# Attention in a macaron block: the probability-value product issued as two halves of 256 query columns

## The chip, the cores and the metric

The kernel runs on one core of one Trainium2 chip. The metric is the device time of the whole program in microseconds (us), the median of several runs. Engines are written as the profile writes them: PE is TensorE's matmul side and PEld its weight load, DVE is VectorE, ACT is ScalarE, POOL is GpSimd and SP is SyncE, which here only issues DMAs.

## The reference

The program is six stages over 16 sequences of 512 tokens, each token a row of 256 floats: feed-forward, gated linear attention, feed-forward, mixture of experts, **softmax attention with 16 heads**, mixture of experts. Only the fifth stage is touched:

```python
q = q.reshape(B, S, 16, 16).transpose(0, 2, 1, 3)      # k, v alike
scores = jnp.einsum('bhsd,bhtd->bhst', q, k) / math.sqrt(16)
scores = scores + _band_mask(S, scores.dtype)          # 0.1 where |s - t| <= 2
attn = jax.nn.softmax(scores, axis=-1)
out = jnp.einsum('bhst,bhtd->bhsd', attn, v)
```

followed by the output projection and the residual sum.

## The kernel before

The attention stage is `att_stage` (line 962). Every engine has its own instruction stream, written out by hand, and semaphores tie the streams together. All streams loop over the 16 sequences with `over_sequences`: the first and the last sequence are written out, the 14 between them are a loop. One sequence is 16 **steps** (`st`), four heads by one tile of 128 keys; four steps make a **group** of four heads (`GROUPS`, `GH`, `TILES` are all 4). A step is four **pairs** (`i` = 0 to 3, one for each head). A pair on PE is

- `s2_unit` (matmul on line 1229): the transposed scores, 128 keys by 512 queries, of this step, into one of two PSUM buffers `s2_`. It waits until ACT has read the buffer of the head two before;
- `s1_unit` (line 1217): scores of the step seven ahead (`AHEAD`), wanted only for their row maximum, into one of two buffers `s1_`. It waits until DVE has read the buffer two before.

ACT takes the exponential of every `s2_` buffer into `prob` (`exp_unit`, line 1382), DVE the maximum of every `s1_` buffer (`max_unit`, line 1476). When the four exponentials of a step are there, POOL multiplies the band's factor into them (`band_factor`, line 1134). The **product** `pv` (matmul on line 1250) then multiplies the four heads' probabilities (128 keys by 512 queries each, float32) by their values and a column of ones, 32 columns of weights for each head, each head in its own quarter of the PE's columns, so that the four run beside each other. It accumulates over the four steps of a group in the bank `pv`. The product of step `st - 1` stands behind pair 3 of step `st`:

```python
if i == 3 and st:
    pv(b, st - 1)
```

`prob` has two buffers; `exp_unit` of pair 0 waits for the product of two steps before. After a group ACT copies `pv` out (`ot_copy`, line 1362, at pair 0 of steps 1, 5, 9, 13), PE transposes it (`out_t`, line 1263) and DVE normalises it.

Between the pairs PE also does the projections of the next sequence and of the last one, at places given by tables of (step, pair): `XT_AT` transposes, `QK_AT` the projections of queries and keys (line 1189, three matmuls at each place: one in step 3, three in 4, three in 8, one in 9), `OT_AT` and `Y_AT` the output projection (steps 6, 10, 11), `V_AT` the values (line 1198, six matmuls at each place: steps 13, 14, and two in 15). In a pair these come behind the product. The projected queries and keys go through ACT (`k_full`, `high_part`), POOL (`low_part`, line 1143) and SP (`write`, line 1064) to DRAM, and from there back into stacks (`load`, line 1075). The row maxima of a group are transposed (`max_t`, line 1239, at pair 1 of steps 1, 5, 9, 13), copied by ACT and put into the query stack by a DMA (`max_row`, line 1080); pair 0 of steps 0, 4, 8 and 12 waits for it. On SP's queue the `max_row` for step 8 stands behind the `write` of the next sequence's first half, and the one for step 12 behind the `write` of its second half.

Of the kernel before, what the change touches and what calls it, by code (L numbers as in the profile page):

```python
# [17 lines left out]
TILES = TOKENS // P  # L18
DM = 256
# [927 lines left out]
HD = DM // HEADS  # L947
GROUPS, GH = 4, 4
STEPS = GROUPS * TILES
# [12 lines left out]
def att_stage(core, a, name):  # L962
# [6 lines left out]
    nc, s = core.nc, core.sem  # L969
    SCALE = HD ** -0.5  # L970
    WIDE = P + 2 * BAND
    with ExitStack() as ctx:
# [22 lines left out]
        vaug = core.sbuf("v_ones", [P, TILES, HEADS, 2 * HD], F32, ctx)  # L995
        prob = core.sbuf("prob", [P, 2, GH, TOKENS], F32, ctx)
# [9 lines left out]
        pvp = core.psum("pv", [P, TOKENS], ctx)  # L1006
# [12 lines left out]
        band_done = s(name + "_band_done")  # L1019
        pv_done = s(name + "_pv_done")  # L1020
# [5 lines left out]
        ot_ready = s(name + "_ot_ready")  # L1026
# [8 lines left out]
        v_ready = s(name + "_v_ready")  # L1035
# [6 lines left out]
        first = lambda b: isinstance(b, int) and b == 0  # L1042

        with nc.Block() as block:
# [121 lines left out]
            def _(pe):  # L1166
                pe.wait_ge(spread_done, 2)
                n = 0
                for x, w in ((bvs, "h"), (bvs, "l"), (bvl, "h")):
                    for k in range(KT):  # L1170
                        op = nc.tensor.matmul(tpy[:, 0, :], x[:, k, :], (wh if w == "h" else wl)["o"][:, k, :],
                                              start=(n == 0), stop=(n == 5))
# [4 lines left out]
                def qk_proj(b, m, parts=range(4), after_o=False):  # L1177

                    if parts[0] == 0 and m == 0:
                        pe.wait_ge(norm.xl_ready, b + 1)  # L1180
                    elif parts[0] == 0:
                        pe.wait_ge(full_ready, 2 * (KT * b + m))
                        if after_o:
                            pe.wait_ge(ol_ready, b - 1)
                    for part in parts:
                        x, k = part // 2, part % 2
                        n = "qk"[x]
                        for i, (w, act) in enumerate([(wh, core.xh), (wl, core.xh), (wh, core.xl)]):
                            op = nc.tensor.matmul(tp[:, x, :], w[n][:, k, m * P:(m + 1) * P], act[:, k, :],
                                                  start=(k == 0 and i == 0), stop=(k == KT - 1 and i == 2))  # L1190
                    if parts[-1] == 3:
                        op.then_inc(qk_ps, 1)
# [17 lines left out]
                def s1_unit(b, st, i):  # L1210

                    g, qt = st // TILES, st % TILES
                    if qt == 0 and i == 0:
                        pe.wait_ge(loaded[g], PER_LOAD * b + PER_LOAD)
                    pe.wait_ge(max_done, (b * STEPS + st) * GH + i + 1)
                    r = slice(0, MAX_ROW)
                    nc.tensor.matmul(s1p[i % 2][:, :], qs[r, g, i, qt * P:(qt + 1) * P], ks[r, g, i, :],  # L1217
                                     start=True, stop=True).then_inc(s1_ready, 1)

                def s2_unit(b, st, i):  # L1220

                    g, kt = st // TILES, st % TILES
                    if kt == 0 and i == 0:
                        pe.wait_ge(rowed[g], 16 * b + 16)
                    pe.wait_ge(exp_done, (b * STEPS + st) * GH + i + 1)
                    r = slice(0, MAX_ROW + 1)
                    nc.tensor.matmul(s2p[i % 2][:, :], ks[r, g, i, kt * P:(kt + 1) * P], qs[r, g, i, :],  # L1229
                                     start=True, stop=True).then_inc(s2_ready, 1)  # L1230

                def max_t(b, g):
                    pe.wait_ge(max_done, (b * GROUPS + g) * TILES * GH + TILES * GH + 2)

                    if first(b) and g in (1, 2):
                        pe.wait_ge(nmt_ready, g)
                    elif not (first(b) and g == 0):
                        pe.wait_ge(on_ready, b * GROUPS + g - 2)
                    nc.tensor.transpose(mp[0:TILES * GH, 0:P], nm[:, g % 2, :, :].rearrange("p h t -> p (h t)"),
                                        core.ident[:, :]).then_inc(nm_ready, 1)  # L1240

                def pv(b, st):
                    g, kt = st // TILES, st % TILES
                    pe.wait_ge(band_done, b * STEPS + st + 1)
                    if st == 0:
                        pe.wait_ge(v_ready, b + 1)
                    if kt == 0 and not (first(b) and g == 0):
                        pe.wait_ge(ot_ready, b * GROUPS + g)
                    for i in range(GH):
                        op = nc.tensor.matmul(pvp[2 * HD * i:2 * HD * (i + 1), :], vaug[:, kt, GH * g + i, :], prob[:, kt % 2, i, :],  # L1250
                                              start=(kt == 0), stop=(kt == TILES - 1))
                    op.then_inc(pv_done, 1)

                def out_t(b, g):

                    pe.wait_ge(ot_ready, b * GROUPS + g + 1)

                    if isinstance(b, int) and b == core.batches - 1 and g >= 2:
                        pe.wait_ge(on_ready, b * GROUPS + g)
                    else:  # L1260
                        pe.wait_ge(nmt_ready, b * GROUPS + g + 3)
                    for qt in range(TILES):
                        op = nc.tensor.transpose(mp[:, qt * P:(qt + 1) * P], ot[:, qt * P:(qt + 1) * P], core.ident[:, :])
                    op.then_inc(tr_ready, 1)
# [11 lines left out]
                def o_project(b, t):  # L1276
                    if t == 0:
                        pe.wait_ge(ol_ready, b + 1)
                    tokens(t, oh, ol, "o", y_ps)
# [12 lines left out]
                def body(b, before, more):  # L1292
                    for st in range(STEPS):
                        ahead = st + AHEAD
                        for i in range(GH):
                            s2_unit(b, st, i)
                            if ahead < STEPS:
                                s1_unit(b, ahead, i)
                            elif more:
                                s1_unit(b + 1, ahead - STEPS, i)  # L1300

                            at = (st, i)
                            if i == 3 and st:
                                pv(b, st - 1)
                            elif i == 3 and before:
                                pv(b - 1, STEPS - 1)
                            if st % TILES == 1 and i == 1:
                                if st + TILES < STEPS:
                                    max_t(b, st // TILES + 1)
                                elif more:  # L1310
                                    max_t(b + 1, 0)
                            if st % TILES == 2 and i == 0:
                                if st > 2:
                                    out_t(b, st // TILES - 1)
                                elif before:
                                    out_t(b - 1, GROUPS - 1)
                            if more and at in XT_AT:
                                n = XT_AT.index(at)
                                norm.transpose(pe, b + 1, lambda: pe.wait_ge(v_ready, b + 1), range(n, n + 1))
                            if more and at in QK_AT[0]:  # L1320
                                n = QK_AT[0].index(at)
                                qk_proj(b + 1, 0, range(n, n + 1))
                            if more and at in QK_AT[1]:
                                n = QK_AT[1].index(at)
                                qk_proj(b + 1, 1, range(n, n + 1), before)
                            if before and at in OT_AT:
                                if more:
                                    o_transpose(b - 1, OT_AT.index(at), full_ready, 2 * (KT * b + KT + 1))
                                else:
                                    o_transpose(b - 1, OT_AT.index(at), v_ready, b + 1)  # L1330
                            if before and at in Y_AT:
                                o_project(b - 1, Y_AT.index(at))
                            if more and at in V_AT:
                                v_proj(b + 1, V_AT.index(at), before)

                over_sequences(pe, core.batches, body)
                last = core.batches - 1
                pv(last, STEPS - 1)
                out_t(last, GROUPS - 1)
                for k in range(KT):  # L1340
                    o_transpose(last, k, *((y_ready, last + 1) if last else (v_ready, 1)))
# [880 lines left out]
```

## Time and profile before

| | us |
|---|---|
| median of 3 runs (4211.86 to 4222.06) | 4212.57 |
| the profiled execution's own time | 4213.35 |
| its span, first to last instruction | 4211.6 |
| attention: from the first s2 matmul (2177.6) to the last (3439.5) | 1262 |
| one sequence in the middle of it, by its 16 steps | 79.2 |
| PE busy over the whole span | 3768.9 (89%) |

A row of the timeline has the start in us, the duration in us, engine, line, operation, tiles and shapes, and, where the engine had been idle, how long and what ended it. A matmul's duration overlaps the next one's, so the distance from start to start tells what a matmul costs. A float32 matmul of the product appears as two records. The granted TensorE clock (PEclk) is either 1.00 (2.4 GHz) or 0.50 (1.2 GHz); a mean between them is a stretch with both.

### The profile page before, as it was taken

How to read it: one execution, taken by the hardware profiler on the slowest of the kernel's cores; microseconds unless marked ns; L12 is line 12 of the kernel's file. 1: busy time of each engine (PE TensorE's matmuls, PEld its weight loads, DVE VectorE, ACT ScalarE, POOL GpSimd, SP SyncE). 2: the span in 40 equal slices, each digit the busy share in tenths (PEclk: the TensorE clock that was granted, in tenths of full speed). 3: DMA queues.
4: the chain of work that ended last, by engine and by line, in shares of the span. 5: the costliest groups of instructions: out<-in, count | busy, mean ns of one | idle time of the engine just before them, and what ended most of it. 6: DMA issues, size and time to landing. Idle time of an engine off the chain costs nothing. (4 is left out here: it accounts for less than half of the span.)

```text
span 4211.6 us, 79961 instructions
## 1 busy us (share of the span) xinstructions
PE 3768.9 (89%) x27516; PEld 2923.9 (69%) x27516; DVE 2720.6 (65%) x5626; ACT 1790.0 (43%) x3205; POOL 1364.4 (32%) x1045
## 2 busy tenths in 40 slices
PE   6997888887997999999968899998999979999999
PEld 4886677776886888888734455554555538888888
DVE  5665677775676566666655666666676655666665
ACT  3444344443554333333325555555555553333333
POOL 2555222222665222222222323323323322222222
PEclk9998999998998999999969999999999989999999
DMA  3000000000001000000034334333333410000000
GB/s 101 0 0 14 2 0 0 0 0 1 0 0 38 1 0 0 0 0 0 10 69 90 76 67 90 83 68 86 86 68 83 90 46 6 15 10 10 15 10 16
DMA packets 72273, 131.72 MB, mean 31 GB/s; under 512 B 7776, under 2 KB 40944, under 8 KB 66048
## 3 DMA queue, kind: packets, MB, share of 16 engines
q1 hardware_dynamic: 72192, 130.65, 13.2%
q8 instruction: 49, 0.80, 0.1%
q14 instruction: 32, 0.26, 0.0%
HBM read 71.38 MB, written 58.72 MB: 31 GB/s over the span
## 5 line engine op out<-in xcount | busy, mean ns | idle before, releaser
L1476 DVE TENSOR_REDUCE neg_max_sb<-s_ps 128x1 f32<-128x512 f32 x1024 | 689.5, 687 | 436.0 <-PE s_ps L1217 433.1
L1382 ACT ACTIVATE prob_sb<-s_ps 128x512 f32<-128x512 f32 x1024 | 599.8, 599 | 543.4 <-PE s_ps L1229 532.7
L850 POOL TENSOR_TENSOR m_act_lo_sb<-m_act_sb,m_act_hi_sb 128x512 fp32r<-128x512 f32 x320 | 414.1, 1294 | 1042.1 <-ACT m_act_hi_sb L816 1042.1
L806 ACT ACTIVATE m_silu_sb<-moe_h_ps 128x512 f32<-128x512 f32 x320 | 191.4, 598 | 966.7 <-PE moe_h_ps L761 966.7
L1229 PE MATMUL s_ps<-q_stack_sb,k_stack_sb 97*128 97x512 f32 x1024 | 483.3, 473 | 101.5 <-DMA q_stack_sb<-neg_max_t_sb 87.2
L1134 POOL TENSOR_TENSOR prob_sb<-prob_sb,band_sb 128x520 f32<-128x520 f32 (+1 forms) x256 | 285.2, 1114 | 853.0 <-ACT prob_sb L1382 852.9
L904 DVE TENSOR_TENSOR m_act_sb<-moe_h_ps,m_silu_sb 128x512 f32<-128x512 f32 x320 | 220.6, 689 | 502.1 <-ACT m_silu_sb L806 472.4
L1229 PEld LDWEIGHTS s_ps<-q_stack_sb,k_stack_sb 97*128 97x128 f32 x1024 | 203.0, 199 | 409.4 <-ACT prob_sb L1382 239.1
L1217 PE MATMUL s_ps<-k_stack_sb,q_stack_sb 96*128 96x512 f32 x1024 | 451.8, 444 | 28.7 <-DMA k_stack_sb<-qk_scratch 16.3
L529 POOL TENSOR_TENSOR f_sq_lo_sb<-f_sq_sb,f_sq_hi_sb 128x512 fp32r<-128x512 f32 x256 | 329.6, 1296 | 349.8 <-ACT f_sq_hi_sb L504 349.7
L916 DVE SCALAR_TENSOR_TENSOR x_resident_sb<-moe_y_ps,gates_sb,x_resident_sb 128x256 f32 (+1 forms) x1024 | 422.5, 474 | 0.5
L779 PE MATMUL moe_y_ps<-w2h_sb,m_act_hi_sb 128*128 128x256 f32 x1280 | 367.2, 287 | 12.3 <-DVE x_resident_sb L916 10.0
L779 PE MATMUL moe_y_ps<-w2h_sb,m_act_lo_sb 128*128 128x256 f32 x1280 | 358.4, 280 | 0.0
L779 PE MATMUL moe_y_ps<-w2l_sb,m_act_hi_sb 128*128 128x256 f32 x1280 | 358.4, 280 | 0.0
L499 ACT ACTIVATE f_relu_sb<-ffn_hp_ps 128x512 f32<-128x512 f32 x256 | 153.4, 599 | 314.1 <-PE ffn_hp_ps L452 313.6
L1250 PE MATMUL pv_ps<-prob_sb,v_ones_sb 128*32 128x512 f32 x2048 | 282.1, 624 | 3.5 <-POOL prob_sb L1134 1.5
L1217 PEld LDWEIGHTS s_ps<-k_stack_sb,q_stack_sb 96*128 96x128 f32 x1024 | 208.1, 203 | 100.5 <-DVE neg_max_sb L1476 50.6
L779 PEld LDWEIGHTS moe_y_ps<-w2h_sb,m_act_hi_sb 128*128 128x128 f32 x1280 | 240.6, 188 | 37.1 <-DVE x_resident_sb L916 21.0
L761 PE MATMUL moe_h_ps<-xnT_hi_sb,w1h_sb 128*128 128x512 f32 x640 | 259.9, 406 | 4.7 <-DVE xnT_lo_sb L158 4.7
L566 DVE TENSOR_TENSOR f_sq_sb<-ffn_hp_ps,f_relu_sb 128x512 f32<-128x512 f32 x256 | 174.8, 687 | 134.3 <-ACT f_relu_sb L499 99.2
L761 PE MATMUL moe_h_ps<-xnT_hi_sb,w1l_sb 128*128 128x512 f32 x640 | 259.4, 405 | 0.0
L761 PE MATMUL moe_h_ps<-xnT_lo_sb,w1h_sb 128*128 128x512 f32 x640 | 257.9, 403 | 0.0
(282 smaller groups left out, 8904.4 us busy)
## 6 DMA issues: line engine op xcount, KB each, us to landing
qk_scratch<-qk_hi_sb SPq DMA_DIRECT2D x128, 256.0 KB
q_stack_sb<-qk_scratch SPq DMA_DIRECT2D x64, 384.0 KB, 5.2
k_stack_sb<-qk_scratch SPq DMA_DIRECT2D x64, 384.0 KB, 7.0
qk_scratch<-qk_lo_sb SPq DMA_DIRECT2D x64, 256.0 KB
x_resident_sb<-x SPq DMA_DIRECT2D x4, 2048.0 KB, 17.8
out<-x_resident_sb SPq DMA_DIRECT2D x16, 512.0 KB, 2.9
moe_w_values_sb<-routed_w SPq DMA_DIRECT2D x12, 512.0 KB, 6.5
moe_w_values_sb<-shared_w SPq DMA_DIRECT2D x6, 256.0 KB, 5.4
```

Of the source, the lines that this page charges most:

```text
L529: nc.gpsimd.tensor_tensor(sql[:, j, :], sq[:, j % 2, :], as_f32(sqh[:, j, :]), ALU.subtract).then_inc(low_ready, 1)
L761: op = nc.tensor.matmul(out[e % 2][:, :], w[:, e, k, :], x[:, k, :], start=(k == 0 and i == 0), stop=(k == KT - 1 and i == 2))
L779: op = nc.tensor.matmul(y[:, t, :], x[:, slot(e), t * P:(t + 1) * P], w[:, e, :], start=(e <= EXPERTS and t % 2 == 0 and i == 0), stop=(i ...
L850: nc.gpsimd.tensor_tensor(al[:, slot(e), :], act_f[:, e % 2, :], as_f32(ah[:, slot(e), :]), ALU.subtract).then_inc(low_ready, 1)
L904: nc.vector.tensor_tensor(act_f[:, e % 2, :], h3[e % 2][:, :], silu[:, e % 2, :], ALU.mult).then_inc(act_ready, 1)
L916: op = nc.vector.scalar_tensor_tensor(xt, y[:, t, :], gain, xt, ALU.mult, ALU.add)
L1134: nc.gpsimd.tensor_tensor(pr, pr, bcast(band[:, off:off + hi - lo].unsqueeze(1), [P, GH, hi - lo]), ALU.mult).then_inc(band_done, 1)
L1217: nc.tensor.matmul(s1p[i % 2][:, :], qs[r, g, i, qt * P:(qt + 1) * P], ks[r, g, i, :], start=True, stop=True).then_inc(s1_ready, 1)
L1229: nc.tensor.matmul(s2p[i % 2][:, :], ks[r, g, i, kt * P:(kt + 1) * P], qs[r, g, i, :], start=True, stop=True).then_inc(s2_ready, 1)
L1250: op = nc.tensor.matmul(pvp[2 * HD * i:2 * HD * (i + 1), :], vaug[:, kt, GH * g + i, :], prob[:, kt % 2, i, :], start=(kt == 0), stop=(kt ...
L1382: nc.scalar.activation(prob[:, kt % 2, i, :], s2p[i % 2][:, :], ACT.Exp).then_inc(exp_done, 1)
L1476: nc.vector.tensor_reduce(nm[:, g % 2, i, qt:qt + 1], s1p[i % 2][:, :], AXIS_X, ALU.max, negate=True).then_inc(max_done, 1)
```

## The change

The product is issued in two calls. The first, `half` 0, takes query columns 0 to 255 and stands behind pair 2; the second, columns 256 to 511, stands behind pair 3. The waits are on the first call, the semaphore increment on the second. Each call has four matmuls of 256 columns where there were four of 512. The accumulation's start flag is set by the first half of a group's first step only.

```diff
-                def pv(b, st):
+                def pv(b, st, half):
                     g, kt = st // TILES, st % TILES
-                    pe.wait_ge(band_done, b * STEPS + st + 1)
-                    if st == 0:
-                        pe.wait_ge(v_ready, b + 1)
-                    if kt == 0 and not (first(b) and g == 0):
-                        pe.wait_ge(ot_ready, b * GROUPS + g)
+                    c = slice(half * DM, half * DM + DM)
+                    if half == 0:
+                        pe.wait_ge(band_done, b * STEPS + st + 1)
+                        if st == 0:
+                            pe.wait_ge(v_ready, b + 1)
+                        if kt == 0 and not (first(b) and g == 0):
+                            pe.wait_ge(ot_ready, b * GROUPS + g)
                     for i in range(GH):
-                        op = nc.tensor.matmul(pvp[2 * HD * i:2 * HD * (i + 1), :], vaug[:, kt, GH * g + i, :], prob[:, kt % 2, i, :],
-                                              start=(kt == 0), stop=(kt == TILES - 1))
-                    op.then_inc(pv_done, 1)
+                        op = nc.tensor.matmul(pvp[2 * HD * i:2 * HD * (i + 1), c], vaug[:, kt, GH * g + i, :],
+                                              prob[:, kt % 2, i, c], start=(kt == 0 and half == 0),
+                                              stop=(kt == TILES - 1), skip_group_check=True)
+                    if half:
+                        op.then_inc(pv_done, 1)
...
-                            if i == 3 and st:
-                                pv(b, st - 1)
-                            elif i == 3 and before:
-                                pv(b - 1, STEPS - 1)
+                            if i >= 2 and st:
+                                pv(b, st - 1, i - 2)
+                            elif i >= 2 and before:
+                                pv(b - 1, STEPS - 1, i - 2)
```

On PE, in step 4 of a middle sequence, from pair 2 to the first score matmul of step 5, the program before has (s_0 and s_1 are the two buffers of either kind of scores, tp is the projection's bank):

```order
L1229 MATMUL s_0_ps<-q_stack_sb,k_stack_sb 128x512
L1215 REGISTER_ALU
L1217 MATMUL s_0_ps<-k_stack_sb,q_stack_sb 128x512
L1189 MATMUL tp_ps<-xnT_hi_sb,Wk_hi_sb 128x512
L1189 MATMUL tp_ps<-xnT_hi_sb,Wk_lo_sb 128x512
L1189 MATMUL tp_ps<-xnT_lo_sb,Wk_hi_sb 128x512
L1227 REGISTER_ALU
L1229 MATMUL s_1_ps<-q_stack_sb,k_stack_sb 128x512
L1215 REGISTER_ALU
L1217 MATMUL s_1_ps<-k_stack_sb,q_stack_sb 128x512
L1250 MATMUL pv_ps<-prob_sb,v_ones_sb 32x512 x4
```

At the same place on PE the changed program has (line 1252 is the product's matmul there):

```order
L1229 MATMUL s_0_ps<-q_stack_sb,k_stack_sb 128x512
L1215 REGISTER_ALU
L1217 MATMUL s_0_ps<-k_stack_sb,q_stack_sb 128x512
L1252 MATMUL pv_ps<-prob_sb,v_ones_sb 32x256 x4
L1189 MATMUL tp_ps<-xnT_hi_sb,Wk_hi_sb 128x512
L1189 MATMUL tp_ps<-xnT_hi_sb,Wk_lo_sb 128x512
L1189 MATMUL tp_ps<-xnT_lo_sb,Wk_hi_sb 128x512
L1227 REGISTER_ALU
L1229 MATMUL s_1_ps<-q_stack_sb,k_stack_sb 128x512
L1215 REGISTER_ALU
L1217 MATMUL s_1_ps<-k_stack_sb,q_stack_sb 128x512
L1252 MATMUL pv_ps<-prob_sb,v_ones_sb 32x256 x4
```

The first half has moved ahead of the third place's projection and of pair 3; the second half stands where the whole product stood. No other engine's stream is changed.

## Rows read from the trace of the kernel before

**Rows 1.** The page: PE's busy time, and the product's group of instructions.

```profile
PE 3768.9 (89%) x27516; PEld 2923.9 (69%) x27516; DVE 2720.6 (65%) x5626; ACT 1790.0 (43%) x3205; POOL 1364.4 (32%) x1045
...
L1250 PE MATMUL pv_ps<-prob_sb,v_ones_sb 128*32 128x512 f32 x2048 | 282.1, 624 | 3.5 <-POOL prob_sb L1134 1.5
```

**Rows 2.** Timeline of PE alone, end of step 14 and start of step 15.

```profile
2815.16 0.40 PE L1229 MATMUL s_ps<-q_stack_sb,k_stack_sb 97*128 97x512 f32 x1
2815.40 0.39 PE L1217 MATMUL s_ps<-k_stack_sb,q_stack_sb 96*128 96x512 f32 x1
2815.72 1.06 PE L1250 MATMUL pv_ps<-prob_sb,v_ones_sb 128*32 128x512 f32 x8
2816.72 0.50 PE L1229 MATMUL s_ps<-q_stack_sb,k_stack_sb 97*128 97x512 f32 x1
2817.06 0.39 PE L1217 MATMUL s_ps<-k_stack_sb,q_stack_sb 96*128 96x512 f32 x1
```

**Rows 3.** Timeline of a step with nothing but pairs and product (last sequence).

```profile
3395.79 0.61 PE L1250 MATMUL pv_ps<-prob_sb,v_ones_sb 128*32 128x512 f32 x4
...
3396.33 0.50 PE L1229 MATMUL s_ps<-q_stack_sb,k_stack_sb 97*128 97x512 f32 x1
...
3396.87 2.34 ACT L1382 ACTIVATE prob_sb<-s_ps 128x512 f32<-128x512 f32 x4 [1.18 <-PE s_ps L1229]
...
3397.10 2.57 DVE L1476 TENSOR_REDUCE neg_max_sb<-s_ps 128x1 f32<-128x512 f32 x4 [0.97 <-PE s_ps L1217]
...
3397.52 0.50 PE L1229 MATMUL s_ps<-q_stack_sb,k_stack_sb 97*128 97x512 f32 x1
...
3397.86 0.49 PE L1217 MATMUL s_ps<-k_stack_sb,q_stack_sb 96*128 96x512 f32 x1
...
3398.18 0.39 PE L1229 MATMUL s_ps<-q_stack_sb,k_stack_sb 97*128 97x512 f32 x1
...
3398.45 0.49 PE L1217 MATMUL s_ps<-k_stack_sb,q_stack_sb 96*128 96x512 f32 x1
...
3398.87 1.06 PE L1250 MATMUL pv_ps<-prob_sb,v_ones_sb 128*32 128x512 f32 x8
...
3399.87 0.50 PE L1229 MATMUL s_ps<-q_stack_sb,k_stack_sb 97*128 97x512 f32 x1
```

**Rows 4.** Busy time by step: steps 0, 1, 3, 4, 12, 14, and all 16 summed.

```profile
2742.07:2745.93 3.86, 3.61 (x20) 1.58 (x16) 3.08 (x6) 2.18 (x4) 1.53 (x2) 1.00 0.96 170
2745.93:2750.51 4.58, 4.20 (x25) 2.02 (x22) 3.88 (x7) 3.83 (x10) 0.67 (x2) 1.00 0.09 14
...
2754.45:2759.20 4.75, 4.54 (x24) 2.07 (x20) 4.20 (x8) 2.52 (x5) 1.57 (x2) 1.00 0.00 0
2759.20:2764.38 5.18, 5.18 (x29) 3.29 (x25) 2.96 (x5) 2.92 (x5) 1.10 (x2) 1.00 0.00 0
...
2803.79:2808.37 4.58, 4.58 (x16) 2.15 (x16) 2.77 (x4) 2.39 (x4) 0.99 (x1) 0.63 0.85 152
...
2812.50:2816.72 4.22, 4.22 (x31) 2.70 (x27) 3.30 (x7) 2.28 (x4) 1.10 (x2) 1.00 0.00 0
...
sum 79.16, PE 72.02 PEld 40.45 DVE 53.15 ACT 44.83 POOL 24.92; mean PE 4.50 PEld 2.53 DVE 3.32 ACT 2.80 POOL 1.56
```

**Rows 5.** Timeline of PE: first matmuls of steps 8 and 12, and a wait in step 9.

```profile
2779.97 0.50 PE L1229 MATMUL s_ps<-q_stack_sb,k_stack_sb 97*128 97x512 f32 x1 [2.66 <-DMA q_stack_sb<-neg_max_t_sb]
...
2787.47 0.50 PE L1217 MATMUL s_ps<-k_stack_sb,q_stack_sb 96*128 96x512 f32 x1 [0.29 <-DMA k_stack_sb<-qk_scratch]
...
2803.79 0.50 PE L1229 MATMUL s_ps<-q_stack_sb,k_stack_sb 97*128 97x512 f32 x1 [2.60 <-DMA q_stack_sb<-neg_max_t_sb]
```

**Rows 6.** Timeline of SP's DMA issues in steps 6 and 7.

```profile
2771.89 3.13 SPq L1064 DMA_DIRECT2D qk_scratch<-qk_lo_sb  x2
2775.15 0.96 SPq L1080 DMA_DIRECT2D q_stack_sb<-neg_max_t_sb  x1
```

**Rows 7.** Timeline of POOL: the band factor of step 5, in step 6.

```profile
2770.65 1.13 POOL L1134 TENSOR_TENSOR prob_sb<-prob_sb,band_sb 128x528 f32<-128x528 f32 x1
```

In rows 4 the columns are the stretch in us, its length, the busy us of PE, PEld, DVE, ACT and POOL with the number of instructions of each, the granted clock, the share of the DMA engines and GB/s.

More of the change, by code:

```diff
@@ L1337, in _ @@
                 last = core.batches - 1
-                pv(last, STEPS - 1)
+                pv(last, STEPS - 1, 0)
+                pv(last, STEPS - 1, 1)
                 out_t(last, GROUPS - 1)
```

## The prediction

> **What bounds the kernel now.** The page first: PE is busy 89% of the span, and the product has 282.1 us of it in 2048 records [rows 1]. That says where the change sits, not what it is worth, so next the attention stage step by step. The busy times by step [rows 4] show PE at 72.02 us of a sequence's 79.16, and two kinds of step: in steps 4 and 14 PE is busy from end to end, in steps 0 and 1 it isn't, and DVE and ACT have extra work. Then the timeline at the steps' ends. The reader should see two things there. First, around each product PE takes longer than its columns need [rows 2]. Second, steps 8 and 12 begin with a wait of 2.66 and 2.60 us for the DMA that brings the row maxima [rows 5], and this DMA stands on SP's queue behind the write of the next sequence's projections [rows 6]. What PE does in the steps just before such a wait is hidden by it; what it does elsewhere sets the time.
>
> **What a product costs PE, whole and halved.** Start to start, an ordinary score matmul takes 0.24 us (2815.16 to 2815.40). Around the product: 0.32 from the last s1 matmul to the product, 1.00 from there to the next s2 matmul, and 0.34 from that to its s1 matmul, whose weight load isn't hidden as usual [rows 2]. Together 1.66, less the 0.48 of two ordinary distances: a whole product costs 1.18 us. Its second record begins 0.54 before the next s2 matmul (3395.79 to 3396.33) [rows 3], so the first pass over 512 columns takes 1.00 - 0.54 = 0.46. The second pass streams as many columns, of which half are to go as well; it is drawn at 0.43 here, a little under the first (its start isn't delayed by a weight load). A half product then streams about 0.43 us less than a whole one: 1.00 - 0.43 = **0.57 from its start to the next s2 matmul**. Everything else around it comes once for each call: 0.32 + 0.57 + 0.34 - 0.48 = 0.75. Two halves cost 1.50 where the whole cost 1.18: **+0.32 us a step where PE sets the pace**. No trace of before shows 256 columns. The bound below is that all of the 1.00 halves (0.50, and 2 x 0.68 = 1.36: +0.18). The bound above is that nothing but the first pass's 0.46 and half as much of the second go (0.65: +0.4 or more); I take 0.57, as rows 2 and 3 give it.
>
> What the rows show is that PE stands still on the way into and out of the four-quarter layout. The Trainium skill has a rule for this, and it speaks against the change: TensorEngine Tiling (Array Packing), section Key Properties, says that changing the tiling mode drains the TensorE, while different tiles of one mode work in parallel. TensorE: Matmul & The Clock Gate puts a warm matmul's constant part at 166 ns; two drains more for each step would be an estimated 0.33 us, where the rows give 0.32.
>
> **Can the split pay for this by keeping ACT and DVE fed?** That is the change's possible gain: behind each whole product ACT waits 1.18 and DVE 0.97 us [rows 3]. I walk through the plain step, whose first s2 matmul is at 0. Before [rows 3]: s2 of pair 2 at 1.19 (it waits for ACT's first exponential), s1 at 1.53, pair 3 at 1.85 and 2.12, product at 2.54, next step at 3.54. After: pairs 0 to 2 as before, s1 of pair 2 at 1.53, half product at 1.53 + 0.42 = 1.95 (0.42 is the distance 3398.45 to 3398.87), s2 of pair 3 at 2.52, its s1 at 2.86, second half at 2.86 + 0.32 = 3.18, next step at 3.75. So **+0.21** instead of +0.32: only 0.1 of PE's waits in pair 3 is filled. ACT and DVE do wait less at a time, but they aren't what sets the pace (2.34 and 2.57 us for the four).
>
> **The sequence, step by step.** I count from one DMA wait to the next.
> - Steps 13, 14, 15 and 4: PE is busy throughout (14 and 4 in [rows 4]): 4 x 0.32 = 1.28.
> - Steps 2 and 3: PE 4.54 of 4.75 in step 3, with one short wait for DVE's low part, which itself comes later since DVE's maxima do: 2 x 0.32 = 0.64, a little less if the half product falls into that wait.
> - Steps 0 and 1: DVE's normalisation delays the maxima (3.08 and 3.88 busy), ACT has the copies (3.83 in step 1) [rows 4]. In step 0 the split gives 0.07 to 0.1 back (the first half runs where pair 3 waited for DVE); in step 1 the plain step's 0.2 comes on top: together 0.15.
> - Step 12 has no extra work, at the half clock for most of its 4.58 us (mean 0.63) [rows 4]: 0.2 to 0.6, taken as 0.3.
> - Step 8: PE-bound at +0.32, but PE then waits 0.29 in step 9 for the key stack's load [rows 5], which hides most of it: 0.1.
> - Steps 5 to 7 and 9 to 11: nothing. The chain that ends at steps 8 and 12 is ACT's high part, POOL, SP's write (3.13 for its last two) and the row DMA (0.96 to issue) [rows 6], which PE doesn't touch after step 5 and 9. PE's extra 1.0 to 1.3 us goes into the 2.66 and 2.60 [rows 5]. Were that cover gone, these six steps would cost 6 x 0.32 = 1.9 us a sequence. In step 6 the earlier place has a price of its own: POOL finishes the band factor of step 5 only at 2771.78 [rows 7], so the first half waits about 1.1 us, and behind it pair 3 and the transposes; this too ends in the wait before step 8.
>
> Sum: 1.28 + 0.64 + 0.15 + 0.3 + 0.1 = 2.47 us a sequence, for 15 sequences 37. The last one has plain steps and no DMA waits of this kind: nine steps at 0.21 and seven without s1 matmuls at nearly nothing, 2. Together +39. The extra weight loads and the four more instructions a step have no cost beyond the measured distances, and the other stages are untouched. The profiled execution took 4213.35, which gives 4252; it stands 0.8 above the median of the runs: **4251**.
>
> **The rivals.**
> - **The halves are cheap, and the split feeds ACT and DVE (faster).** It decides at the distance from a half product's start to the next s2 matmul: below 0.41 us a PE-bound step gains (2 x (x + 0.18) against 1.18), below 0.46 the plain one. At 0.35 they gain 0.12 and 0.23; nine exposed steps at 0.16 on average give 1.4 a sequence, 23 in all: 4190. For it: ACT's and DVE's waits. Against: it needs more than the streaming to shrink, and the overhead of 0.3 around each product is there at each of them.
> - **The clock stays up (still slower, by less).** The granted clock is at 1.2 GHz for part of steps 8 and 12, after PE's waits. The split shortens these waits by 1.0 to 1.3 us, perhaps to where the clock no longer falls. Step 12 would lose its 4.58 - 3.54 = 1.0 us; step 8 gains little, as the load in step 9 ends at the same time. 15 x 1.0 off: 4236; half of the sequences: 4243. The Trainium skill's page TensorE: Matmul & The Clock Gate (The HAM clock gate) has the half rate come after idleness only; by that rule alone a shorter wait would keep the clock in part of the sequences. The trace has no such shorter wait to show it.
> - **Nothing is hidden (slower by more).** All 256 steps at 0.32 are 82 us: 4295. For this the chain to the row DMA would have to move with PE, through ACT's work in step 5.
> - **The change doesn't move the time**: PE's waits in the exposed steps would have to take in all of it; [rows 4] shows them full.
>
> **How the numbers follow.** The forecast, +20 to +60, has 0.62; the clock staying up, 0.13, of which a third ends near no change; nothing hidden 0.10; the cheap halves 0.09; no difference 0.06. About 0.3% (12.6 us) is what a measurement of this kernel can tell from no change. So slower 0.81, same 0.11, faster 0.08. The range leaves out the cheap halves and the top of the worst case: 4214 to 4290.
>
> **What would show it.** In the changed trace: the distance from a half product to the next s2 matmul, 0.57; a plain step at 3.75; steps 4 and 14 at 5.5 and 4.54; the waits before steps 8 and 12 shorter by 1.0 to 1.3 us; the product's first half in step 6 waiting for POOL; a middle sequence at 81.6 us. The prediction is wrong if that distance is under 0.46, if the waits before steps 8 and 12 stay as long, or if the clock's half-rate stretches vanish.

## The result, and the profile after

| | before | after |
|---|---|---|
| median of the runs, us | 4214.43 (4 runs, 4211.86 to 4222.06) | 4263.35 (4 runs, 4253.89 to 4267.32) |
| ratio to before | | 1.011, 95% interval 1.0087 to 1.0133 |
| the profiled execution: its own time / its span | 4213.35 / 4211.6 | 4267.32 / 4265.6 |
| attention, from its first s2 matmul to the last step's first | 1260.2 | 1320.5 |
| a middle sequence, mean of the 14 | 80.2 | 84.0 |

The change makes the kernel 49 us slower, 1.1%. The forecast was 4251, slower by 37 to 39. (The profiled execution of after is the longest of its four, 4 us over their median.) In the two profiled executions the attention stage alone grew by 60 us, and the stages outside it, whose code is the same, took 6 us less; so what is read from steps of the profile doesn't add up to the 49 us exactly. The page of the changed kernel has, as lines for rows 1:

```profile
PE 3839.6 (90%) x29564; PEld 2952.3 (69%) x29564; DVE 2719.3 (64%) x5626; ACT 1796.4 (42%) x3205; POOL 1362.7 (32%) x1045
...
L1252 PE MATMUL pv_ps<-prob_sb,v_ones_sb 128*32 128x256 f32 x4096 | 349.0, 415 | 18.3 <-POOL prob_sb L1134 18.2
```

PE is busy for 71 us more, 67 of them in the product, with the same number of columns multiplied (a part of the 71 is the lower clock shown below). DVE and ACT do what they did.

The end of step 14 and the start of step 15 in a middle sequence, PE alone, as the line for rows 2:

```profile
2844.17 0.40 PE L1217 MATMUL s_ps<-k_stack_sb,q_stack_sb 96*128 96x512 f32 x1
2844.50 0.64 PE L1252 MATMUL pv_ps<-prob_sb,v_ones_sb 128*32 128x256 f32 x8
2845.07 0.50 PE L1229 MATMUL s_ps<-q_stack_sb,k_stack_sb 97*128 97x512 f32 x1
2845.40 0.40 PE L1217 MATMUL s_ps<-k_stack_sb,q_stack_sb 96*128 96x512 f32 x1
```

From the last s1 matmul to the half product 0.33, from there to the next s2 matmul 0.57, and to its s1 matmul 0.33. In rows 2 the whole product has 0.32, 1.00 and 0.34. The distances on the way in and on the way out are as long around 256 columns as around 512.

The plain step, against rows 3, in the last sequence (PE; the rows of ACT and DVE are from the same stretch's views of these engines):

```profile
3450.90 0.50 PE L1229 MATMUL s_ps<-q_stack_sb,k_stack_sb 97*128 97x512 f32 x1
...
3452.09 0.50 PE L1229 MATMUL s_ps<-q_stack_sb,k_stack_sb 97*128 97x512 f32 x1
3452.43 0.49 PE L1217 MATMUL s_ps<-k_stack_sb,q_stack_sb 96*128 96x512 f32 x1
3452.85 0.64 PE L1252 MATMUL pv_ps<-prob_sb,v_ones_sb 128*32 128x256 f32 x8
3453.42 0.50 PE L1229 MATMUL s_ps<-q_stack_sb,k_stack_sb 97*128 97x512 f32 x1
3453.75 0.40 PE L1217 MATMUL s_ps<-k_stack_sb,q_stack_sb 96*128 96x512 f32 x1
3454.08 0.64 PE L1252 MATMUL pv_ps<-prob_sb,v_ones_sb 128*32 128x256 f32 x8
3454.65 0.50 PE L1229 MATMUL s_ps<-q_stack_sb,k_stack_sb 97*128 97x512 f32 x1
```

```profile
3451.44 1.79 ACT L1387 ACTIVATE prob_sb<-s_ps 128x512 f32<-128x512 f32 x3 [0.63 <-PE s_ps L1229]
3453.95 0.60 ACT L1387 ACTIVATE prob_sb<-s_ps 128x512 f32<-128x512 f32 x1 [0.73 <-PE s_ps L1229]
```

```profile
3451.67 1.98 DVE L1481 TENSOR_REDUCE neg_max_sb<-s_ps 128x1 f32<-128x512 f32 x3 [0.54 <-PE s_ps L1217]
3454.19 0.69 DVE L1481 TENSOR_REDUCE neg_max_sb<-s_ps 128x1 f32<-128x512 f32 x1 [0.54 <-PE s_ps L1217]
```

The step takes 3454.65 - 3450.90 = 3.75 us; in rows 3 it took 3.54. ACT waits 0.63 and 0.73 us where it had waited 1.18 once, and DVE 0.54 twice for 0.97 once. So the split does feed them more evenly, and it buys 0.1 us: the step is 0.21 longer, where a step with PE busy throughout is 0.3 longer. Most of the second call's price stays, as PE sets the pace.

One middle sequence by stretches, against rows 4. The changed kernel first: steps 0, 1, 3, 4; then 5 to 7, 8 to 11, 12, 13, and 14 with 15 (columns as in rows 4).

```profile
2765.43:2769.18 3.75, 3.69 (x28) 1.67 (x24) 3.20 (x8) 2.28 (x4) 1.10 (x2) 1.00 1.01 177
2769.18:2773.98 4.80, 4.16 (x33) 2.08 (x29) 3.58 (x6) 3.82 (x10) 1.11 (x2) 1.00 0.18 27
2778.28:2783.32 5.04, 4.62 (x31) 2.23 (x27) 4.27 (x9) 2.28 (x4) 1.10 (x2) 1.00 0.00 0
2783.32:2788.83 5.51, 5.51 (x37) 3.37 (x33) 2.77 (x5) 2.50 (x5) 1.12 (x2) 1.00 0.00 0
2788.83:2804.34 15.51, 12.59 (x89) 6.35 (x85) 10.51 (x18) 9.69 (x19) 6.79 (x5) 1.00 0.31 102
2804.34:2828.43 24.09, 21.75 (x138) 13.35 (x138) 13.05 (x21) 11.35 (x21) 6.82 (x5) 0.93 0.62 131
2828.43:2834.46 6.03, 6.03 (x25) 2.65 (x25) 2.77 (x4) 2.39 (x4) 0.66 (x1) 0.50 0.78 130
2834.46:2840.49 6.03, 6.03 (x36) 3.21 (x32) 2.54 (x4) 3.02 (x6) 2.81 (x3) 0.66 0.01 1
2840.49:2849.91 9.42, 9.42 (x74) 5.86 (x71) 7.65 (x20) 4.67 (x8) 2.24 (x3) 1.00 0.00 0
```

The same stretches of the kernel before, from steps 5 to 7 on:

```profile
2764.38:2779.97 15.59, 12.18 (x65) 5.94 (x61) 10.26 (x17) 9.28 (x19) 6.37 (x5) 1.00 0.32 101
2779.97:2803.79 23.82, 20.93 (x106) 13.02 (x106) 13.13 (x21) 11.35 (x21) 6.84 (x5) 0.93 0.61 132
...
2808.37:2812.50 4.13, 4.13 (x28) 2.32 (x24) 2.67 (x4) 2.77 (x6) 2.92 (x3) 1.00 0.17 24
2812.50:2821.23 8.73, 8.73 (x59) 5.68 (x55) 7.46 (x19) 4.57 (x8) 2.25 (x3) 1.00 0.05 8
```

The reader should see three things. Steps 5 to 7 and 8 to 11 are as long as before within 0.3 us: the wait for the DMA chain at their end takes in what PE has more. Steps 3, 4, 14 and 15 are each 0.3 us longer at the full clock. And step 13 is 1.9 us longer with a mean granted clock of 0.66, where it had 4.13 us and 1.00: the half clock that follows the wait before step 12 lasts through step 12 and most of step 13.

### The profile page after: what moved, and what is told of

The parts are those of the page before. It is cut to its first block and busy times, and to the rows that moved or that the text cites. A ratio compares the mean times of both kernels' runs of the same rounds, so it can differ in the third digit from the quotient of the medians.

```text
span 4265.6 us, 84057 instructions
## 1 busy us (share of the span) xinstructions
PE 3839.6 (90%) x29564; PEld 2952.3 (69%) x29564; DVE 2719.3 (64%) x5626; ACT 1796.4 (42%) x3205; POOL 1362.7 (32%) x1045
## 5 line engine op out<-in xcount | busy, mean ns | idle before, releaser
L1229 PE MATMUL s_ps<-q_stack_sb,k_stack_sb 97*128 97x512 f32 x1024 | 496.9, 486 | 73.5 <-DMA q_stack_sb<-neg_max_t_sb 61.4
L1252 PE MATMUL pv_ps<-prob_sb,v_ones_sb 128*32 128x256 f32 x4096 | 349.0, 415 | 18.3 <-POOL prob_sb L1134 18.2
```

The source lines that it names most:

```text
L1252: op = nc.tensor.matmul(pvp[2 * HD * i:2 * HD * (i + 1), c], vaug[:, kt, GH * g + i, :], prob[:, kt % 2, i, c], start=(kt == 0 and half == 0),
```

## The experiments

For each stretch I give the mean over the 14 middle sequences, from the distances between the steps' first s2 matmuls. In this table the last three columns are runs described below. The last row is the whole attention stage of the profiled execution, from its first s2 matmul to the last step's first; it has the first and the last sequence too.

| us | before | after | before, three fills | after, three fills | after, two fills |
|---|---|---|---|---|---|
| steps 0 to 4 | 22.37 | 23.41 | 22.38 | 23.41 | 23.40 |
| steps 5 to 7 | 15.55 | 15.54 | 15.58 | 15.52 | 15.52 |
| steps 8 to 11 | 24.30 | 24.32 | 24.14 | 24.21 | 25.01 |
| step 12 | 4.98 | 5.28 | 3.55 | 3.75 | 3.72 |
| step 13 | 4.29 | 6.08 | 4.13 | 4.46 | 4.47 |
| steps 14, 15 | 8.73 | 9.42 | 8.73 | 9.40 | 9.42 |
| sequence | 80.2 | 84.0 | 78.5 | 80.8 | 81.5 |
| at the half clock | 9.0 | 11.7 | 0 | 0 | 2.4 |
| attention stage | 1260.2 | 1320.5 | 1238.4 | 1273.4 | 1283.4 |

### The cut without the second entry

From the changed kernel:

```diff
-                            if i >= 2 and st:
-                                pv(b, st - 1, i - 2)
-                            elif i >= 2 and before:
-                                pv(b - 1, STEPS - 1, i - 2)
+                            for half in range(2 if i == 3 else 0):
+                                if st:
+                                    pv(b, st - 1, half)
+                                elif before:
+                                    pv(b - 1, STEPS - 1, half)
```

> The product is cut into the two halves of 256 columns, but both stand behind pair 3, one right after the other: the cut without the second entry into the four-quarter layout. Theory (the cost is PE standing still on the way in and out, 0.32 us for each further call between other matmuls): the pair of calls takes about 1.0 to 1.05 us to the next s2 matmul instead of 1.00; time within 12 us of the kernel before, 4212 to 4226. Rival (halves are dear in themselves, by more instructions and shorter streams): the pair takes 1.14 us or more, and the time rises by at least half of the change's 49 us, to 4240 or more.

Measured: 4213.72 (10 runs) against 4214.49, ratio 1.000 (0.999 to 1.0009). PE's timeline has both calls as one row:

```profile
2816.79 0.40 PE L1217 MATMUL s_ps<-k_stack_sb,q_stack_sb 96*128 96x512 f32 x1
2817.12 1.07 PE L1252 MATMUL pv_ps<-prob_sb,v_ones_sb 128*32 128x256 f32 x16
2818.12 0.50 PE L1229 MATMUL s_ps<-q_stack_sb,k_stack_sb 97*128 97x512 f32 x1
```

Sixteen records of 256 columns take the 1.00 us that eight of 512 took. Twice as many instructions and weight loads cost nothing as long as the layout stays; the rival falls.

### The earlier place without the cut

From the kernel before:

```diff
-                            if i == 3 and st:
+                            if i == 2 and st:
                                 pv(b, st - 1)
-                            elif i == 3 and before:
+                            elif i == 2 and before:
```

> The whole product, not cut, behind pair 2 instead of pair 3: the earlier place alone. Theory (the place costs only the wait for POOL's band factor in step 6, which the wait before step 8 hides): within 15 us of the kernel before, 4205 to 4230, step 6 longer by about 1.2 us and step 7 shorter by as much, no rise in step 13 beyond 0.4 us. Rival (the earlier place delays exponentials and projections behind it, and this is where part of the 49 us is): 4230 to 4250, with steps 4, 8 and 13 longer.

Measured: 4264.97, ratio 1.0113 (1.0095 to 1.0131). The theory was wrong here: for a whole product the place alone costs as much as the change does. But it costs in other steps. Steps 4 and 14 stay at 5.19 and 4.24 us (before 5.19 and 4.23), where the change adds 0.3 to each. What rises is step 3 (6.0 for 4.76), step 15 with 0 (8.8 for 8.4), 1 (4.95 for 4.59), 5 (4.20 for 3.83), 6 and 7 together, and steps 8 to 12. Step 3 in this kernel, all engines but PEld and POOL:

```profile
2779.36 0.68 DVE L158 TENSOR_TENSOR xnT_lo_sb<-tp_ps,xnT_hi_sb 128x512 fp32r<-128x512 f32 x1
...
2779.50 0.49 PE L1217 MATMUL s_ps<-k_stack_sb,q_stack_sb 96*128 96x512 f32 x1 [1.09 <-DVE neg_max_sb L1476]
...
2779.92 1.06 PE L1250 MATMUL pv_ps<-prob_sb,v_ones_sb 128*32 128x512 f32 x8
...
2780.92 0.50 PE L1189 MATMUL tp_ps<-xnT_hi_sb,Wq_hi_sb 128*128 128x512 f32 x1
...
2782.17 1.09 ACT L1382 ACTIVATE prob_sb<-s_ps 128x512 f32<-128x512 f32 x2 [3.12 <-PE s_ps L1229]
```

Here PE waits 1.09 us for a maximum, since DVE has its extra work at pair 3 of step 2 and pair 0 of step 3 and gets pair 3's scores only after the product. Behind the wait come product and projection in a row, and ACT is without scores for 3.12 us.

### Product and projections change places

```diff
-QK_AT = [[(3, 2), (4, 0), (4, 1), (4, 2)], [(8, 0), (8, 1), (8, 2), (9, 0)]]
-OT_AT = [(6, 1), (6, 2)]
-Y_AT = [(10, 0), (10, 1), (10, 2), (11, 0)]
-V_AT = [(13, 2), (14, 1), (15, 0), (15, 2)]
+QK_AT = [[(3, 3), (4, 0), (4, 1), (4, 3)], [(8, 0), (8, 1), (8, 3), (9, 0)]]
+OT_AT = [(6, 1), (6, 3)]
+Y_AT = [(10, 0), (10, 1), (10, 3), (11, 0)]
+V_AT = [(13, 3), (14, 1), (15, 0), (15, 3)]
```

on top of the kernel just described.

> The whole product behind pair 2, as in the run before that took 4265, and now the pieces of projections that stood behind pair 2 in steps 3, 4, 6, 8, 10, 13 and 15 stand behind pair 3: product and projections have changed places. First reading (the earlier place costs 50 us because the product stacks onto a projection, 1.7 to 2 us in a row, and ACT and DVE have only two buffers of scores to work on): most of the loss goes, 4205 to 4230, steps 3 and 15 back to under 5.1 and 4.8. Rival (the place itself costs, by the band factor's wait and by later exponentials): 4245 to 4270.

Measured: 4254.53, ratio 1.0100 (1.0083 to 1.0117). Neither reading holds. Of the 50 us, 10 come back, in step 5 (3.65 for 4.20) and, with 0.1 to 0.2 each, steps 0, 3, 8 to 11 together, 12 and 13, so the stacking is a small part. Step 15 stays at 5.21 and step 3 at 5.78. In both DVE has other work around pair 3 and the next pair 0 (statistics in steps 14 and 15, the low part in 2 and 3), which fits the wait shown above, but no run took that work away, and the rest of this cost stays open.

### Keeping the clock up

```diff
+                def filler(b, st, n):
+                    pe.wait_ge(on_ready, b * GROUPS + st // TILES)
+                    for _ in range(n):
+                        nc.tensor.matmul(mp[:, :], wh["q"][:, 0, 0:P], wh["k"][:, :, :].rearrange("p k m -> p (k m)"),
+                                         start=True, stop=True)
...
+                            if more and at in ((7, 3), (11, 3)):
+                                filler(b, st, 10 if st == 7 else 10)
```

The extra matmuls' result is used by nobody; the kernel computes what it did. They stand in the first and the 14 middle sequences. First in the kernel before, with ten behind step 7 and ten behind step 11:

> The kernel before with ten more score-like matmuls of 512 columns (2.4 us) on PE behind steps 7 and 11 of the 14 middle sequences and of the first, into a PSUM bank that is free there, so that PE is busy while it waits for the row maxima. Theory (the granted clock falls to 1.2 GHz after these waits, and costs 1.0 to 1.4 us in step 12 and 13; in step 8 nothing, since step 9 then waits for the key stack): the half-clock time in steps 8 to 13 goes to nearly nothing, a middle sequence takes 78.8 us instead of 80.2, the whole 4190 to 4200. Rival (the clock costs nothing here, other engines set the pace): 4205 to 4225, same or slower by the extra matmuls.

Measured: 4192.89, ratio 0.9947 (0.9931 to 0.9964). Step 12 takes 3.54 us and the sequence 78.7, with 0.5 us at the half clock instead of 9.0. Then in the changed kernel, whose waits are shorter, with 6 and 8 extra matmuls:

> The changed kernel with six such extra matmuls behind step 7 and eight behind step 11. Theory (of the 4.0 us that a middle sequence lost, 1.5 are the half clock that lasts through step 13, and 2.4 are the second entry and exit of each product where PE sets the pace): step 13 falls from 6.1 to 4.5 us and step 12 from 5.3 to 3.9, the whole to 4212 to 4226, that is 24 to 32 us above the kernel before with the same fill. Rival (step 13 is long because the earlier half waits for something): step 13 stays at 5.5 us or more, and the whole at 4240 to 4265.

Measured: 4235.23, ratio 1.0052 (1.0035 to 1.0069). Step 13 falls to 4.47, 0.34 over its partner: what it had lost beyond that was the clock. The rival that it waits for something falls. But the whole is 42 us above its partner and not 24 to 32, and the table shows where: steps 8 to 11 are 0.7 us longer than before, with 2.4 us at the half clock in step 9. There PE waits for the key stack's load: wherever it waits for it, in either kernel, with extra matmuls or without, the load ends the wait 7.3 to 8.0 us after step 8 begins. The next pair of runs puts seven extra matmuls behind step 8 as well (before: 10, 7 and 10; changed: 6, 7 and 8). In both the extra matmuls' semaphore wait is changed too, to one group earlier for the new place; for the two old places it is the same. The changed kernel's edit, without that line:

```diff
-                            if more and at in ((7, 3), (11, 3)):
-                                filler(b, st, 6 if st == 7 else 8)
+                            if more and at in ((7, 3), (8, 3), (11, 3)):
+                                filler(b, st, {7: 6, 8: 7, 11: 8}[st])
```

> The changed kernel with extra matmuls behind steps 7 and 11 as in the run that took 4235, and seven more behind step 8, ahead of step 9's wait for the key stack. Theory (with the clock up everywhere, what is left of the change is 0.3 us in each of nine steps, 2.3 us a sequence; the 0.7 us in steps 8 to 11 comes from a clock that falls in step 9's wait): steps 8 to 11 go from 25.0 to 24.4 us a sequence, the whole to 4222 to 4230. Rival (the 0.7 us are switches after all, in steps 10 and 11): 4232 to 4240, steps 8 to 11 stay at 25.0.

> The kernel before with the extra matmuls behind steps 7, 8 and 11: the partner of the run above, and a candidate for the fastest. Theory: the clock fell in step 9 in a few sequences only, so 4188 to 4194, against 4193 without the third place; and 33 to 38 us below its partner. Rival: the third place's 1.7 us run over the wait and cost 0.3 us or more a sequence, 4196 to 4202.

Measured: 4224.43 (10 runs), ratio 1.0019 (1.001 to 1.0029), and 4187.87, ratio 0.9937 (0.992 to 0.9953). The changed kernel and its distance to its partner are where they were expected. Both profiles show the full clock throughout the 14 middle sequences. One sequence of each, steps 0 to 4, 12, 13 and 14 with 15. The changed kernel with three fills:

```profile
2742.09:2765.52 23.43, 22.34 (x150) 11.79 (x146) 16.61 (x29) 14.15 (x29) 5.57 (x6) 1.00 0.19 34
...
2805.23:2808.98 3.75, 3.75 (x25) 1.67 (x25) 2.44 (x4) 2.28 (x4) 0.03 (x1) 1.00 0.80 149
2808.98:2813.45 4.47, 4.47 (x36) 2.47 (x32) 2.67 (x5) 2.77 (x6) 3.45 (x3) 1.00 0.36 53
2813.45:2822.86 9.41, 9.41 (x75) 5.87 (x71) 7.65 (x20) 4.67 (x8) 2.24 (x3) 1.00 0.00 0
```

The kernel before with three fills:

```profile
2729.27:2751.65 22.38, 21.59 (x109) 11.34 (x106) 16.87 (x29) 14.49 (x29) 5.58 (x6) 1.00 0.19 33
...
2791.38:2794.91 3.53, 3.53 (x16) 1.55 (x16) 2.57 (x4) 2.24 (x4) 0.57 (x1) 1.00 0.81 146
2794.91:2799.05 4.14, 4.14 (x27) 2.32 (x24) 2.67 (x4) 2.78 (x6) 3.33 (x3) 1.00 0.47 67
2799.05:2807.79 8.74, 8.74 (x59) 5.69 (x55) 7.46 (x19) 4.57 (x8) 2.25 (x3) 1.00 0.03 5
```

The two differ by 36.6 us. That is the change almost without the clock (the first sequence of either still has 10.2 us at the half clock): 2.25 us a middle sequence, of which 1.03 is in steps 0 to 4, 0.20 in 12, 0.33 in 13, 0.67 in 14 and 15, and nothing beyond 0.1 in steps 5 to 11. The rest is what the split adds at the half clock, and its size depends on where it is read. By the medians of whole runs it is 49 - 37 = 12 us. In the profiled attention stages, where alone the kernels differ, it is (1320.5 - 1260.2) - (1273.4 - 1238.4) = 25 us, or 1.6 us in each middle sequence and 3 in the first. The two don't agree because the untouched stages of the profiled executions differ by some us, and the runs of one kernel by up to 13; 12 to 25 us is what can be said. The kernel before with three fills is the fastest here, 27 us (0.63%) below the kernel before.

### The cut at column 32

The changed kernel with two fills, cut elsewhere:

```diff
-                    c = slice(half * DM, half * DM + DM)
+                    c = slice(32, TOKENS) if half else slice(0, 32)
```

> The changed kernel with the extra matmuls that keep the clock up, and the cut at column 32 instead of 256: the call behind pair 2 takes 32 columns, the one behind pair 3 takes 480. Theory (what a second call costs is the way in and out, whatever its size): its start to the next s2 matmul takes 0.20 us (0.14 and 0.85 for all 512 columns), the other's 0.94; steps 4, 14 and 15 stay at 5.5, 4.57 and 4.85 us as with equal halves, the whole at 4225 to 4240, with the equal halves' 4235. Rival (what costs is product work at the earlier place, where it stands on top of projections and leaves ACT and DVE without scores): with a sixteenth of the product there, steps 4, 14 and 15 go back to 5.2, 4.25 and 4.5, the whole to 4193 to 4205, as the uncut kernel with extra matmuls.

Measured: 4237.05, ratio 1.0053 (1.0036 to 1.007), where the equal halves had 4235.23. PE in step 15:

```profile
2750.49 0.39 PE L1217 MATMUL s_ps<-k_stack_sb,q_stack_sb 96*128 96x512 f32 x1
2750.80 0.27 PE L1252 MATMUL pv_ps<-prob_sb,v_ones_sb 128*32 128x32 f32 x8
2751.00 0.39 PE L1198 MATMUL tp_ps<-Wv_hi_sb,xnT_hi_sb 128*128 128x256 f32 x1
...
2752.39 1.01 PE L1252 MATMUL pv_ps<-prob_sb,v_ones_sb 128*32 128x480 f32 x8
2753.33 0.50 PE L1229 MATMUL s_ps<-q_stack_sb,k_stack_sb 97*128 97x512 f32 x1
```

A call of 32 columns takes 0.20 us to the next matmul and one of 480 takes 0.94, as expected from 0.14 + 0.85 x (share of the 512 columns), which was drawn from the 0.57 of 256 columns and the 1.00 of 512. Steps 4, 14 and 15 are 5.52, 4.56 and 4.84, as with equal halves. So in these steps the price is for the second call, whatever its size, and not for the work at the earlier place. Step 3 is the exception: it is 4.66 us instead of 5.04, less even than the 4.76 of the uncut product, so what the equal halves add there is the work at the earlier place and not the second call. The agreement of the totals is partly luck: what step 3 saves is lost again, as the half clock takes 4.6 us a sequence for 2.4, in steps 9 and 10.

## Why the prediction was right, point by point

- **The price of a call.** Forecast 0.57 from a half product to the next s2 matmul; it is 0.57 at the median of 510 calls. The fixed part, some 0.32 us of PE for each entry, is shown from two sides: no cost when the calls stand together, the same cost at 32 columns. The Trainium skill's rule (TensorEngine Tiling (Array Packing), Key Properties), that a change of tiling mode drains the engine and a change of tile doesn't, agrees with both runs.
- **The plain step.** Forecast 3.75, measured 3.75. Steps 4 and 14: 5.5 and 4.54 forecast, 5.51 and 4.57 measured. The plain step behaves so in steps 0, 3, 4 and 8 of the last sequence.
- **Steps 2 and 3** forecast +0.64, measured +0.62 (4.29 + 5.04 against 3.95 + 4.76). Steps 0 and 1: +0.15 forecast, +0.09 measured, as -0.13 in step 0 and +0.22 in step 1.
- **Nothing in steps 5 to 7 and 9 to 11.** Right for the stretches between the DMA waits: 15.54 for 15.55 and, with step 8, 24.32 for 24.30. Within the second, step 8 is 0.4 us shorter, where +0.1 was forecast, and steps 9 to 11 are 0.4 longer. The first half in step 6 waits for POOL as foreseen; of three middle sequences the view of the waits has (sum, number and mean; PEld's wait begins earlier, PE's own is the 1.1 us of the forecast)

```profile
PEld pv_ps L1252 <- POOL prob_sb L1134: 4.6, 3, 1.5
...
PE pv_ps L1252 <- POOL prob_sb L1134: 3.3, 3, 1.1
```

  and step 6 takes 5.86 us for 4.61, which step 7 gives back (5.90 for 7.11). The wait before step 8 shrank to 1.83 from the 2.66 of rows 5:

```profile
2804.34 0.72 PE L1229 MATMUL s_ps<-q_stack_sb,k_stack_sb 97*128 97x512 f32 x1 [1.83 <-DMA q_stack_sb<-neg_max_t_sb]
```

  That is 0.8 less, where I had said 1.0 to 1.3. Before step 12 it is 2.33 for 2.60 in this sequence, and over the 14 middle sequences the median went from 2.72 to 2.25: only 0.5 less.
- **The sum.** 2.47 a sequence forecast, 2.25 at the full clock, 3.82 with the clock as it was (80.2 to 84.0; the 81.6 of the forecast started from one sequence of 79.2, not from the mean). The last sequence was to cost 2 us and costs nothing (56.9 for 57.0): its steps without s1 matmuls, and steps 1 and 7, gain what the others lose.
- **The term that was mis-sized: the clock.** The sum put step 12 at +0.3 for the half clock and step 13 at a plain +0.32. Measured: +0.30 and +1.79; at the full clock the two are +0.20 and +0.33. I had a rival in which shorter waits keep the clock up. In step 8 that happens in 4 of 14 middle sequences (5.5 us for 7.0), and as said there it brings nothing, because step 9 then waits 1.5 to 1.8 us for the key stack, and in three of the four the clock falls behind that wait. After step 12 the opposite happens: in 10 of the 15 sequences that have the wait, the low clock lasts three times as long as the shortest stretch of before (10.2 us for 3.4; in the kernel before it is 3.4 us in nine sequences and 6.8 in six). No part of the prediction had this. It is 12 us by the medians and 25 by the profiled stages, as worked out above.
- **What was luck.** With 1.57 us a sequence left out, the total is still only 12 us above the forecast. Two terms were a little high (2.47 for 2.25, and 2 us for the last sequence), and where the profiled stage grew by 60 us the whole kernel, by its medians, grew by 49. The price of a call is what the prediction got right; that the total agrees so well is not all due to it.
- **My reading of the place.** "The earlier place has a price of its own" only in step 6, hidden. For the halves this held. For the whole product it doesn't: 50 us. The two costs don't add up to the change, and the change's 37 us at the full clock are not all entries: in step 3, where the cut at column 32 gave 0.38 us back, the rise comes from the place. Why the place costs a whole product so much stays open.

## What to carry to other kernels

Matmuls that use the PE in narrow column groups should stand together: here each entry into that layout and back cost 0.32 us where PE is busy from end to end, at 32, 256 or 480 columns alike, and splitting a call in place cost nothing. Cutting work finer to feed the other engines pays only where they set the pace; ask first in how many steps PE is busy from end to end. Before crediting or blaming an instruction order, look at the granted clock of the same steps: a few otherwise useless matmuls in PE's waits brought 27 us, and none of the orders tried here brought any.

## What the runs showed of the hardware that was not expected

A shorter wait doesn't mean less time at 1.2 GHz. With PE's wait before step 12 cut from 2.72 to 2.25 us (medians of the middle sequences), the time at the half clock went from 9.0 to 11.7 us a sequence, in a stretch where PE is busy from end to end (6.03 of 6.03 us in step 12 and again in 13). During it the half product takes 1.0 us instead of 0.57 to the next matmul. Half products aren't needed for it: the kernel before with three fills, which has whole ones, shows as long a stretch in its first sequence, behind a wait of 2.47 us before step 12:

```profile
2237.75:2247.98 10.23, 10.23 (x36) 5.40 (x35) 5.08 (x8) 4.64 (x10) 1.84 (x2) 0.50 0.42 72
```

What makes it last isn't settled; with extra matmuls in the waits it is gone from the 14 middle sequences of both kernels.
